# A GNN layer kernel: tail rows by SyncE, two tiles gathered raw, another order of scaling, and one loop for the last two batches

## Chip, cores and metric

One core of one Trainium2 chip. The metric is the device time of one execution in microseconds (us); the kernel before was run three times beside its profile.

## What is computed

A graph layer on 6250 nodes of 96 features and 106,250 edges that are sorted by their destination node. E is 830 tiles of 128 edges and a tail of 10.

```python
h = relu(layernorm(x))                                  # 6250 x 96
ea = edge_attr @ W_edge.T + b_edge                      # 106250 x 96
msg = relu(h[src] + ea)
aggr = segment_sum(msg, dst, num_segments=6250)
z = relu(((1 + eps) * h + aggr) @ W1.T + b1)
out = x + z @ W2.T + b2
```

## The kernel before

**Tiles and batches.** The 830 tiles are handled in 43 batches: 40 batches of 20 tiles (two sides of 10), then END with 16, LATE with 10 and LAST with 4. A side is a run of consecutive tiles; since edges are sorted, the nodes of one side fit into a window of 128 nodes or a few of them. For every tile three things come together: edge features (TensorE, in `edge_features_by_feature`, L505, for most batches, and in `edge_features`, L526, for the first and the last two), rows of the source nodes (a gather by GpSimd, L375), and a 0/1 matrix that says which edge goes to which node of the window (`make_select`, L771, on VectorE). For most batches the edge features come out transposed. ScalarE moves 32-wide blocks of them (`move_blocks`, L451), VectorE transposes within the blocks (`turn_blocks`, L926), adds the gathered rows (`add_rows`, L941), and takes the message apart into three bf16 parts with ScalarE's help (L458, L920, L463, L955). TensorE sums the messages by node (`sum_parts`, L604), and VectorE reduces the three parts (L853) and adds the turned sums of the window before into `acc` (`add_sums`, L825).

**The gathers.** Each gather fetches 128 rows of 384 bytes by a column of `src_all`. For batch 0 they come from `x` itself (20 gathers, in a burst of 13 and one of 7, the second after `norm_ready`), and VectorE normalises the gathered rows ("raw" tiles: `raw_var`, `raw_normalise`, in two parts of 10 tiles, `RAW_PARTS`). All other gathers, 810 and one of 10 rows for the tail (L388), read `h_table`, the normalised rows, which SyncE and ScalarE store to DRAM first; GpSimd waits for all of that store (`table_stored`) before the tail's gather. Two buffers `gathered` take turns. The gathers of batch c wait for two semaphores: `edge_begun` (TensorE's first matmul of features(c-1), which is issued after batch c-2 is used up) and `added` (VectorE's additions of batch c-2, by pairs of groups).

**Orders written out by hand.** Every engine has a program of its own. TensorE does, for each c: `turn_base(c-2)` (L552, for c of 2 to 14 only, which waits for ScalarE's blocks), `sum_windows(c-1)`, features(c+1). VectorE does: additions and parts of batch c, `sum_windows(c-1)`, `turn_blocks(c+1)`. SyncE issues the loads in this order: first source indices, x, weights, edges of batch 0, the table's stores, `dst_by_row`, `dst_all`, the tail's edges, edges of batch 1, five late weights; then, for each c from 2, edges of batch c once features(c-2) are done.

**The start on VectorE.** After the table: `raw_var(0)`; a wait for `dst_by_row` and its minimum (L764); `raw_normalise(0)` (L698, L699, ten of L756, L760); `raw_var(1)`; the maximum (L767); `raw_normalise(1)`. Then batch 0 is added (L941).

**The end.** The matrices of LATE and LAST are made ahead of need (`make_late_select`, L872), and the bounds of END, LATE and LAST are read into registers (nine `value_load`, L834 and L836). VectorE then does `add_rows(LATE)`, `sum_windows(END)`, `add_rows(LAST)`, `add_turned`, and a loop of its own for each of LATE and LAST over their windows, `sum_late_windows`: add two sides (L825), lower the offsets (L840), make the matrix of the next window (L872). TensorE has the matching loops (L613, and L616 for the tail's rows), with a `value_load` ahead of each. Then the two layers of the MLP follow in ten blocks of 625 nodes: z (L650), ReLU on ScalarE (L482), the result (L667), x added on VectorE (L997), stores (L361). TensorE's L650 of block 1 stands behind waits for `select_made` and both `late_selected` semaphores, since it writes the bank (`const_ps`) from which these matrices are made.

The sides' windows in this data end after one pass of each of the late loops.

```python
            for c in range(1, BATCHES):
                if c >= SLOTS:
                    pool.wait_ge(edge_begun, c)
                for p, (k0, k1) in enumerate(pairs[c]):
                    last_use = used_by(c, p, SLOTS)
                    if last_use is not None:
                        pool.wait_ge(added, adds_to[last_use] + p + 1)
                    for k in range(k0, k1):
                        gather(h_table, c, k)
```

## Time and profile before

| | |
|---|---|
| median of 3 runs | 1225.51 us (1225.41 to 1225.88) |
| the profiled execution | 1224.89 us |
| its span in the trace | 1223.1 us |
| granted TensorE clock, mean of the span | 0.673 of 2.4 GHz |
| busy: PE, VectorE, ScalarE, GpSimd | 41%, 50%, 42%, 64% of the span |
| HBM read, written | 87.85 MB, 4.80 MB |

The profiled execution's own time stands 1.8 us above its span and 0.6 us below the median. In the rows of the trace a line reads: start, duration, engine, line of the kernel, operation, written tile <- read tiles, shapes, count, and in brackets the idle time of the engine ahead of it and who ended that. "issue" means that nothing in the profile ended the wait, "remote" that a semaphore moved which the trace ties to no instruction close by. Rows of the same line that follow each other are merged. The duration of a DMA_INDIRECT row on POOL is what GpSimd is recorded to spend on issuing it, not its transfer.

### The profile page before, as it was taken

The numbers are of one execution on the slowest core, as the hardware profiler recorded it, in microseconds if no ns is written. First come the engines' busy times: TensorE is split into PE (matmuls) and PEld (weight loads), VectorE is DVE, ScalarE is ACT, GpSimd is POOL, SyncE is SP. The second block draws the span as 40 slices with busy tenths as digits, with TensorE's granted clock in tenths as the row PEclk, the third lists the DMA queues.
The fourth block names the chain that finished last, engine by engine and source line by source line (L and its number), as shares of the span: only waits on it lengthen the run. The fifth ranks groups of instructions, "written<-read, shape, count | busy, mean of one in ns | idle before, by whom it ended". The sixth has DMA issues, their size and how long they took to land.

```text
span 1223.1 us, 7306 instructions
## 1 busy us (share of the span) xinstructions
PE 496.0 (41%) x1592; PEld 249.7 (20%) x1592; DVE 607.6 (50%) x739; ACT 518.7 (42%) x713; POOL 785.8 (64%) x838
## 2 busy tenths in 40 slices
PE   2143344344344334245343253442534334425358
PEld 2011111222121112012111121120211111112146
DVE  6665544555554445364536345352545363543563
ACT  5134444344433335353435333343535343433434
POOL 6766666666666666575757575766757575757530
PEclk9967766767767766566666665666656666666669
DMA  7523333222223223242323332322423232322212
GB/s 217 148 66 71 83 78 68 67 68 68 67 67 68 68 68 98 56 112 71 81 71 80 72 79 64 72 68 61 101 54 82 63 72 64 71 64 67 47 28 79
DMA packets 51178, 93.18 MB, mean 76 GB/s; under 512 B 17722, under 2 KB 20443, under 8 KB 51136
## 3 DMA queue, kind: packets, MB, share of 16 engines
q0 software_dynamic: 26592, 40.85, 16.1%
q1 hardware_dynamic: 24390, 51.63, 15.6%
q8 instruction: 14, 0.23, 0.1%
q10 hardware_dynamic: 154, 0.24, 0.1%
q14 instruction: 28, 0.23, 0.1%
HBM read 87.85 MB, written 4.80 MB: 76 GB/s over the span
## 4 chain that ended last, share of the span: by engine, by line
another core or an unknown queue 32%; ACT 23%; issue 21%; DVE 13%; PE 6%; DVEq 4%; DMA 1%; SPq 0%; ACTq 0%
ACT edge_blocks L451 17%; ACT msg_parts L458 3%; DVE turn_ps L941 3%; DVE turn_ps L920 3%; PE turn_ps L505 2%; DVEq L834 2%; DVE turn_ps L926 2%; ACT msg_parts L463 2%; DVE msg_parts L955 1%; PE agg_ps L604 1%; PE turn_ps L667 1%; DVEq L836 1%; DVE stats L705 1%; DVE acc L825 1%
## 5 line engine op out<-in xcount | busy, mean ns | idle before, releaser
L375 POOL DMA_INDIRECT gathered<-h_table,src_all x810 | 764.4, 944 | 382.0 <-issue 237.7
L451 ACT COPY edge_blocks<-turn_ps 32x640 f32<-32x640 f32 (+1 forms) x480 | 325.9, 679 | 475.9 <-remote 358.8
L505 PE MATMUL turn_ps<-edge_in,w_edge 97*96 97x512 f32 x398 | 268.2, 842 | 324.2 <-issue 258.8
L926 DVE STREAM_TRANSPOSE turn_ps<-edge_blocks 128x960 f32<-128x960 f32 (+1 forms) x81 | 89.7, 1153 | 216.4 <-ACT edge_blocks L451 115.8
L853 DVE TENSOR_REDUCE sums<-agg_ps 128x192 f32<-128x576 f32 x41 | 30.9, 753 | 319.8 <-remote 319.8
L505 PEld LDWEIGHTS turn_ps<-edge_in,w_edge 97*96 97x96 f32 x398 | 88.6, 234 | 482.9 <-issue 482.9
L604 PE MATMUL agg_ps<-msg_parts,select 128*128 128x288 bf16 x816 | 155.6, 367 | 0.0
L458 ACT ACTIVATE msg_parts<-turn_ps 128x960 bf16<-128x960 f32 (+1 forms) x83 | 79.2, 957 | 157.2 <-DVE turn_ps L941 110.3
L771 DVE TENSOR_TENSOR select<-const_ps,dst_rel 128x2560 bf16<-128x2560 f32 (+1 forms) x43 | 120.8, 2812 | 33.2 <-issue 28.5
L604 PEld LDWEIGHTS agg_ps<-msg_parts,select 128*128 128x128 bf16 x816 | 103.4, 127 | 46.1
L941 DVE TENSOR_TENSOR turn_ps<-turn_ps,gathered 128x960 f32<-128x960 f32 (+1 forms) x83 | 91.1, 1144 | 2.1 <-DVE gathered L760 0.5
L920 DVE SCALAR_TENSOR_TENSOR turn_ps<-turn_ps,msg_parts 128x960 f32<-128x960 f32 (+1 forms) x83 | 91.1, 1144 | 0.3 <-ACT msg_parts L458 0.3
L955 DVE TENSOR_TENSOR msg_parts<-turn_ps,msg_parts 128x960 bf16<-128x960 f32 (+1 forms) x83 | 90.8, 1136 | 0.3 <-ACT msg_parts L463 0.3
L552 PE MATMUL turn_ps<-ident,h_all 125*96 125x125 f32 x50 | 13.1, 415 | 188.4 <-ACT edge_blocks L451 179.9
L567 PE MATMUL agg_ps<-ident,sums 128*96 128x128 f32 x84 | 23.6, 378 | 150.5 <-DVE acc L825 133.9
L463 ACT CAST msg_parts<-turn_ps 128x960 bf16<-128x960 f32 (+1 forms) x83 | 78.2, 945 | 11.6 <-issue 6.6
L552 PEld LDWEIGHTS turn_ps<-ident,h_all 125*96 125x96 f32 x50 | 7.9, 187 | 199.3 <-issue 199.2
L567 PEld LDWEIGHTS agg_ps<-ident,sums 128*96 128x96 f32 x84 | 10.3, 162 | 174.4 <-issue 171.7
L375 POOL DMA_INDIRECT gathered<-x_dram,src_all x20 | 19.6, 981 | 10.9 <-issue 5.5
L526 PE MATMUL turn_ps<-w_edge,edge_in 97*128 97x96 f32 x68 | 14.4, 406 | 27.1 <-DMA edge_in<-edge_t_dram 14.9
L825 DVE TENSOR_TENSOR acc<-acc,agg_ps 96x128 f32 x84 | 23.4, 279 | 0.9
L526 PEld LDWEIGHTS turn_ps<-w_edge,edge_in 97*128 97x128 f32 x68 | 13.9, 315 | 27.3 <-issue 27.3
(77 smaller groups left out, 187.9 us busy)
## 6 DMA issues: line engine op xcount, KB each, us to landing
edge_in<-edge_t_dram SPq DMA_DIRECT2D x165, 240.0 KB
gathered<-h_table,src_all POOLq DMA_INDIRECT x810
x_all<-x_dram SPq DMA_DIRECT2D x5, 420.0 KB
h_all<-x_dram SPq DMA_DIRECT2D x10, 210.0 KB
out_dram<-h_all SPq DMA_DIRECT2D x10, 210.0 KB
h_table<-h_all SPq DMA_DIRECT2D x3, 420.0 KB
h_table<-h_all SPq DMA_DIRECT2D x1, 630.0 KB
dst_by_row<-dst_rows_dram SPq DMA_DIRECT2D x1, 480.0 KB, 4.1
```

Source lines behind the costliest of these rows:

```text
L375: nc.gpsimd.indirect_dma_start(out=gathered[c % SLOTS][:, at:at + D], out_offset=None, in_=table, in_offset=bass.IndirectOffsetOnAxis(ap=s ...
L451: last = nc.scalar.copy(blocks[e:e + TURN, :, f:f + TURN], edges[f:f + TURN, :, e:e + TURN])
L458: last = nc.scalar.activation(in_parts(msg_parts[c % 2], a, b, 0), in_banks(c, a, b), ACT.Relu)
L463: last = nc.scalar.copy(in_parts(msg_parts[c % 2], a, b, 1), in_banks(c, a, b))
L505: mm = pe.matmul(turn_ps[0:D, q * BANK:q * BANK + (k1 - k0) * EDGE_TILE], w_edge[:], edge_in[c % SLOTS][:, k0 * EDGE_TILE:k1 * EDGE_TILE], ...
L604: mm = pe.matmul(agg_ps[:, s * BANK:s * BANK + SPLIT * D], select[c % 2][:, tile, :], msg_parts[c % 2][:, tile, :, :], start=(t == 0), sto ...
L771: nc.vector.tensor_tensor(select[b][:, 0:tiles, :], iota_ps.unsqueeze(1).broadcast_to((128, tiles, WINDOW)), dst_rel[:, bass.ds(at, tiles) ...
L825: return nc.vector.tensor_tensor(acc[:, cols], acc[:, cols], turned, ALU.add)
L920: return nc.vector.scalar_tensor_tensor(message, message, 0.0, high, ALU.max, ALU.subtract)
L926: last = nc.vector.transpose(in_flat(c, a, b), flat_rows(edge_blocks, a, b))
L941: last = nc.vector.tensor_tensor(put, in_banks(c, a, b), in_rows(gathered[slot], a, b), ALU.add)
L955: last = nc.vector.tensor_tensor(in_parts(msg_parts[c % 2], a, b, 2), in_banks(c, a, b), in_parts(msg_parts[c % 2], a, b, 1), ALU.subtract)
```

## The change

- **Tail rows by SyncE.** The tail's ten source indices come in as an input of their own (`tail_src`), are loaded into SBUF and from there into ten registers of SyncE, and SyncE issues ten DMAs of one row each from `h_table`. They stand behind the late weights and ahead of the edges of batch 2. GpSimd's L388 goes.
- **Two more raw tiles.** The first two tiles of batch 1 are gathered from `x` right behind batch 0's twenty, ahead of the wait for the table's store, and VectorE normalises them (a third raw part of two tiles).
- **Raw scaling ahead of the destinations by row.** VectorE does `raw_normalise(0)` and `raw_var(1)` before it waits for `dst_by_row`.
- **One loop for the last two batches.** LATE and LAST share one loop whose length is the longer of their two spans (one more reduction while the bounds are made); in it TensorE sums LATE, then LAST, and VectorE does the additions and offsets of both and then both comparisons. VectorE reads the bounds of LATE and LAST after `sum_windows(END)`, five loads instead of six.

```diff
-RAW_PARTS = ((0, 10), (10, 20))
+RAW_PARTS = ((0, 10), (10, 20), (20, 22))
+EARLY_TILES = 2
...
-            sp.dma_start(src_all[:, 0:tiles_of[0]], src_tiles[:, 0:tiles_of[0]]).then_inc(src_first_in, 16)
+            sp.dma_start(src_all[:, 0:RAW_TILES], src_tiles[:, 0:RAW_TILES]).then_inc(src_first_in, 16)
...
             load_edges(1)
+            sp.dma_start(tail_index[:], tail_src).then_inc(tail_index_in, 16)
             sp.dma_start(scale_eps[:], eps.rearrange("(a b) -> a b", a=1).broadcast_to((D, 1))).then_inc(late_weights_in, 16)
...
+            tail_row = [sp.alloc_register(f"sp_tail_row{k}") for k in range(TAIL)]
+            sp.wait_ge(tail_index_in, 16)
+            sp.load(tail_row, tail_index[0:1, 0:TAIL])
+            for k in range(TAIL):
+                node = sp.snap(tail_row[k], min_val=0, max_val=N - 1)
+                sp.dma_start(tail_gathered[k:k + 1, :], h_table[bass.ds(node, 1), :]).then_inc(tail_gather_in, 16)
...
             for k in range(FIRST_BURST, tiles_of[0]):
                 gather(x, 0, k)
+            for k in range(EARLY_TILES):
+                gather_early(k)
             pool.wait_ge(src_rest_in, 16)
             pool.wait_ge(table_stored, 16 * len(spread) * len(TABLE_PARTS))
-            nc.gpsimd.indirect_dma_start(
-                out=tail_gathered[:], out_offset=None, in_=h_table,
-                in_offset=bass.IndirectOffsetOnAxis(ap=src_all[0:TAIL, TILES:TILES + 1], axis=0),
-            ).then_inc(tail_gather_in, 16)
...
-                        gather(h_table, c, k)
+                        if c > 1 or k >= EARLY_TILES:
+                            gather(h_table, c, k)
...
-            def sum_late_windows(c):
...
+            def sum_late_windows(span):
                 with pe.Fori(0, span + 1, WINDOW):
+                    this_select = pe.snap(late)
+                    for c in (LATE, LAST):
+                        pe.wait_ge(late_relu_done, c - LATE + 1)
+                        if c == LAST:
+                            pe.wait_ge(tail_relu_done, 1)
+                        pe.wait_ge(late_selected[c], this_select)
+                        sum_rows(c).then_inc(late_summed, 1)
+                    pe.reg_add(window, window, 2)
+                    pe.reg_add(late, late, 1)
...
             raw_var(0)
+            raw_normalise(0)
+            raw_var(1)
             dve.wait_ge(dst_rows_in, 16)
             nc.vector.tensor_reduce(first_last[:, 0:1], dst_by_row[:], AX.X, ALU.min).then_inc(bounds_min_max, 1)
-            raw_normalise(0)
-            raw_var(1)
+            raw_var(2)
             nc.vector.tensor_reduce(first_last[:, 1:2], dst_by_row[:], AX.X, ALU.max).then_inc(bounds_min_max, 1)
-            ordered(raw_normalise(1))
+            raw_normalise(1)
+            ordered(raw_normalise(2))
...
+            def sum_late_windows(firsts, span):
                 with dve.Fori(0, span + 1, WINDOW) as done:
+                    for c in (LATE, LAST):
...
+                        dve.wait_ge(late_summed, this_late)
+                        dve.wait_ge(acc_summed, this_window)
+                        add_sums(0, cols[0], late_sums(c, 0)).then_inc(side_summed, 1)
+                        lower_offsets(first_tile[c], tiles_of[c] + (c == LAST)).then_inc(offsets_made, 1)
+                        dve.wait_ge(side_summed, this_window)
+                        add_sums(1, cols[1], late_sums(c, 1)).then_inc(acc_summed, 1)
+                    lowered, next_window = dve.snap(offsets), dve.snap(window)
                     dve.wait_ge(offsets_made, lowered)
                     dve.wait_ge(acc_summed, next_window)
-                    make_late_select(c)
+                    for c in (LATE, LAST):
+                        make_late_select(c)
...
-            end_bounds, late_bounds, last_bounds = (load_bounds(c) for c in (END, LATE, LAST))
+            end_bounds = load_bounds(END)
             add_rows(LATE)
             sum_windows(END, *end_bounds)
+            late_firsts, joint_span = {c: load_firsts(c) for c in (LATE, LAST)}, load_span(JOINT)
             add_rows(LAST)
             add_turned()
-            sum_late_windows(LATE, *late_bounds)
-            sum_late_windows(LAST, *last_bounds)
+            sum_late_windows(late_firsts, joint_span)
```

**GpSimd's whole program behind its constants**, before (L375 is a gather, L388 the tail's):

```order
L368 AFFINE_SELECT ident<-ident 128x128
L370 IOTA iota_sb 128x128
L375 DMA gathered<-x_dram,src_all 128x96 x20
L388 DMA tail_gathered<-h_table,src_all 10x96
L375 DMA gathered<-h_table,src_all 128x96 x810
```

and in the changed kernel:

```order
L384 AFFINE_SELECT ident<-ident 128x128
L386 IOTA iota_sb 128x128
L391 DMA gathered<-x_dram,src_all 128x96 x20
L398 DMA gathered<-x_dram,src_all 128x96 x2
L391 DMA gathered<-h_table,src_all 128x96 x808
```

The gathers from `h_table` go from 811 to 808, and two stand ahead of them, on the near side of the wait for the table's store.

**VectorE at the start**, before, from the minimum of `dst_by_row` on (`first_last`):

```order
L764 TENSOR_REDUCE first_last<-dst_by_row 96x1
L698 RECIPROCAL rstd<-std 128x10
L699 SCALAR_TENSOR_TENSOR shift<-mean,rstd 128x10
L756 TENSOR_SCALAR gathered<-gathered,rstd,shift 128x96 x10
L760 TENSOR_SCALAR gathered<-gathered 128x960
L745 BN_STATS raw_stats<-gathered 128x6 x10
```

and in the changed kernel, up to the same minimum (its L796) and the new tiles' statistics:

```order
L720 RECIPROCAL rstd<-std 128x10
L721 SCALAR_TENSOR_TENSOR shift<-mean,rstd 128x10
L786 TENSOR_SCALAR gathered<-gathered,rstd,shift 128x96 x10
L790 TENSOR_SCALAR gathered<-gathered 128x960
L771 BN_STATS raw_stats<-gathered 128x6 x10
L711 TENSOR_TENSOR gap<-raw_stats 128x10
L712 TENSOR_TENSOR spread<-raw_stats 128x10
L713 TENSOR_TENSOR mean<-raw_stats 128x10
L714 TENSOR_TENSOR gap<-gap 128x10
L715 SCALAR_TENSOR_TENSOR spread<-gap,spread 128x10
L796 TENSOR_REDUCE first_last<-dst_by_row 96x1
L775 BN_STATS raw_stats<-gathered 128x6 x2
```

The scaling of the first ten tiles and the statistics of the second ten moved ahead of the reduction that waits for `dst_by_row`.

**VectorE in the late loops**, before, from LATE's first addition to LAST's (ISA and REGISTER rows work on registers):

```order
L825 TENSOR_TENSOR acc<-acc,turn_ps 96x128
L840 TENSOR_SCALAR dst_rel<-dst_rel 128x10
L825 ISA
L825 TENSOR_TENSOR acc<-acc,turn_ps 96x128
L872 TENSOR_TENSOR late_select<-const_ps,dst_rel 128x1280
L879 ISA
L879 COMPARE_AND_BRANCH
L879 UNCONDITIONAL_BRANCH
L879 ISA
L828 ISA x2
L825 ISA
L825 TENSOR_TENSOR acc<-acc,turn_ps 96x128
```

and in the changed kernel, from LATE's second addition to the end of the loop's body:

```order
L859 TENSOR_TENSOR acc<-acc,turn_ps 96x128
L918 ISA
L862 ISA
L863 ISA
L859 ISA
L859 TENSOR_TENSOR acc<-acc,turn_ps 96x128
L878 TENSOR_SCALAR dst_rel<-dst_rel 128x5
L859 ISA
L859 TENSOR_TENSOR acc<-acc,turn_ps 96x128
L931 ISA
L910 TENSOR_TENSOR late_select<-const_ps,dst_rel 128x1280
L910 TENSOR_TENSOR late_select<-const_ps,dst_rel 128x640
```

LATE's comparison no longer stands between the additions of LATE and those of LAST; both comparisons stand behind them. On TensorE the second `value_load` and the loop's branch between LATE's matmuls and LAST's go.

## Rows read from the trace of the kernel before

**Rows 1.** The page: the group of the gathers (count; busy, mean ns; idle before)

```profile
L375 POOL DMA_INDIRECT gathered<-h_table,src_all x810 | 764.4, 944 | 382.0 <-issue 237.7
```

**Rows 2.** Timeline of POOL: its waits, with 20 and 40 gathers between them

```profile
120.62 0.94 POOL L375 DMA_INDIRECT gathered<-h_table,src_all  x1 [3.72 <-remote]
...
149.03 0.94 POOL L375 DMA_INDIRECT gathered<-h_table,src_all  x1 [3.75 <-remote]
...
574.47 0.94 POOL L375 DMA_INDIRECT gathered<-h_table,src_all  x1 [6.94 <-remote]
...
630.96 0.94 POOL L375 DMA_INDIRECT gathered<-h_table,src_all  x1 [6.86 <-remote]
```

**Rows 3.** Timeline, 130 to 149 us: TensorE's work and who starts after it

```profile
130.56 3.41 PE L604 MATMUL agg_ps<-msg_parts,select 128*128 128x288 bf16 x20
136.80 4.50 PE L505 MATMUL turn_ps<-edge_in,w_edge 97*96 97x512 f32 x10 [2.82 <-issue]
148.75 0.76 DVE L853 TENSOR_REDUCE sums<-agg_ps 128x192 f32<-128x576 f32 x1 [9.98 <-remote]
```

**Rows 4.** Timeline of POOL, the start and the first two runs of gathers

```profile
23.20 0.94 POOL L375 DMA_INDIRECT gathered<-x_dram,src_all  x1 [4.29 <-DVE shift L699]
26.94 1.54 POOL L375 DMA_INDIRECT gathered<-x_dram,src_all  x1 [0.30 <-issue]
31.28 0.94 POOL L375 DMA_INDIRECT gathered<-x_dram,src_all  x1 [0.30 <-issue]
34.43 0.88 POOL L388 DMA_INDIRECT tail_gathered<-h_table,src_all  x1 [2.21 <-DMA h_table<-h_all]
41.89 1.06 POOL L375 DMA_INDIRECT gathered<-h_table,src_all  x1 [0.30 <-issue]
60.77 0.94 POOL L375 DMA_INDIRECT gathered<-h_table,src_all  x1 [0.30 <-issue]
92.24 0.94 POOL L375 DMA_INDIRECT gathered<-h_table,src_all  x1 [6.81 <-remote]
```

**Rows 5.** Timeline of VectorE and SyncE, 26 to 51 us

```profile
26.75 0.91 DVE L736 TENSOR_SCALAR h_all<-h_all 125x1440 f32<-125x1440 f32 x1
37.67 1.48 DVE L764 TENSOR_REDUCE first_last<-dst_by_row 96x1 f32<-96x1280 int32 x1 [7.62 <-DMA dst_by_row<-dst_rows_dram]
39.30 1.72 SPq L320 DMA_DIRECT2D edge_in<-edge_t_dram  x4
39.52 2.62 DVE L756 TENSOR_SCALAR gathered<-gathered,rstd,shift 128x96 f32<-128x96 f32 x10
42.17 0.66 DVE L760 TENSOR_SCALAR gathered<-gathered 128x960 f32<-128x960 f32 x1
50.73 2.23 DVE L941 TENSOR_TENSOR turn_ps<-turn_ps,gathered 128x960 f32<-128x960 f32 x2 [0.51 <-DVE gathered L760]
```

**Rows 6.** Timeline of TensorE, features of batches 1 and 2

```profile
56.43 4.38 PE L505 MATMUL turn_ps<-edge_in,w_edge 97*96 97x512 f32 x5 [8.46 <-issue]
84.89 7.64 PE L505 MATMUL turn_ps<-edge_in,w_edge 97*96 97x512 f32 x10 [3.04 <-issue]
```

**Rows 7.** Line L834, VectorE's register loads: ns min/median/max, first and last start

```profile
L834 DVEq TENSOR_LOAD <-bounds_i x86: 298/303/547, 71.3 to 1183.5; - x86
```

**Rows 8.** Timeline, the end

```profile
1188.39 5.88 PE L613 MATMUL turn_ps<-late_select,gathered 128*96 128x128 f32 x28 [0.32 <-issue]
1193.92 1.49 DVE L872 TENSOR_TENSOR late_select<-const_ps,dst_rel 128x1280 f32<-128x1280 f32 x1
1195.74 0.28 DVE L825 TENSOR_TENSOR acc<-acc,turn_ps 96x128 f32 x1
1196.13 0.82 DVE L872 TENSOR_TENSOR late_select<-const_ps,dst_rel 128x640 f32<-128x640 f32 x1
1197.39 1.27 PE L650 MATMUL turn_ps<-acc,w 96*96 96x320 f32 x2
```

**Rows 9.** Busy time by stretch: us, PE busy, PEld, DVE, ACT, POOL, PEclk, DMA share, GB/s

```profile
1201.00:1217.00 16.00, 16.00 (x105) 13.03 (x104) 5.23 (x8) 9.94 (x15) 0.00 (x0) 1.00 0.34 106
```

More of the change, by code:

```diff
@@ L560, in _ @@
             selects = pe.alloc_register("pe_selects")
-            late = {c: pe.alloc_register(f"pe_late{c}") for c in (LATE, LAST)}
-            for c in (LATE, LAST):
-                pe.reg_mov(late[c], 1)
+            late = pe.alloc_register("pe_late")
+            pe.reg_mov(late, 1)
             def turn_sums():
@@ L640, in _ @@
                         edge_features(c + 1)
-            sum_late_windows(LAST)
             all_summed = pe.snap(window)
             all_selects = pe.snap(selects)
-            all_late = {c: pe.snap(late[c]) for c in (LATE, LAST)}
+            all_late = pe.snap(late)
             def hidden_sums(c):
```

95 lines of the change are left out of this document (52 added, 43 removed).

## The prediction

> **What bounds the kernel now.** I read the page first, then the timeline of GpSimd (POOL), then that of the other engines over one batch. No engine is busy for two thirds of the span on the page, and the chain of waits gives a third of it to an unknown releaser, so shares don't name the bound; the rhythm does. GpSimd's 810 gathers are 0.944 us each with 0.30 us between them [rows 1], 1.25 us from start to start, without a break over a batch; then it stops for 3.7 us once in 20 gathers, or for 6.9 us once in 40 [rows 2]. The period is 149.03 - 120.62 = 28.41 us for 20 gathers and 630.96 - 574.47 = 56.49 us for 40. Their difference gives 28.08 / 20 = **1.404 us for a gather**, and 28.41 - 28.08 leaves **0.33 us** for a stop. The stops are no slack, then: they are as long as the gathers ahead of them are many, and TensorE's clock and the other engines' work, which differ between the two patterns, do not show in the period.
>
> What ends a stop is odd. VectorE and GpSimd start within 0.3 us, at 148.75 and 149.03 [rows 2, 3], and both wait for TensorE, whose matmuls for them are modelled to have ended by 134.0 and 141.3 [rows 3]. TensorE's signals come when GpSimd's work would be done at 1.404 us a gather. I can't name the mechanism from this trace; I use the rule as measured. It holds at the start too: the first run of gathers begins with the tail's at 34.43 and has 1 + 40; 34.43 + 41 x 1.404 + 0.33 = 92.32, and the row says 92.24 [rows 4]. The Trainium skill (Perfetto Trace Analysis, DMA Instruction, SWDGE) says that the recorded end of such an instruction is when the last DSP has written its descriptors, and that the DSP finishes later. That would allow a true cost above 1.25 us, and the sum by 1.25 would be a gain of 3 x 1.25 instead of 3 x 1.40.
>
> So the forecast is about the number of gathers behind the table's store, and about what happens after the last stop.
>
> **Part 1: gathers.** 811 gathers stand behind the store; 808 will. At 1.404 us that is 4.2 us, if the first run began where it does now. It won't quite: two gathers more stand ahead of it. The burst now ends with the one issued at 31.28, and GpSimd then waits until 34.43 for the store [rows 4]. Two more steps of 1.25 us: the last early gather is issued at 33.78, the run of 38 begins at 35.03. Its stop ends at 35.03 + 38 x 1.404 + 0.33 = 88.7, 3.5 us earlier than 92.24. But if a gather really takes 1.404 us, the seven from 23.20 on and the two new ones carry their arrears into the run: 23.20 + 47 x 1.404 + 0.33 = 89.5, a gain of 2.7 us; and if the 0.6 us by which the gather at 26.94 was held up (1.54 for 0.94) comes on top, 90.1, a gain of 2.1 us. I take **2.7 us**, since the rule fitted every other run with arrears counted, and keep 2.1 and 3.5 as ends.
>
> Every later stop is set by the gathers alone, so this gain travels unchanged to the last one. What could eat it on the way:
>
> - Batch 2's gathers must not find `edge_begun` missing. They follow at 60.77 now and would at about 58. Features(1) begin at 56.43 [rows 6], right behind batch 0's messages. Those come earlier: L756 and L760 of the first ten tiles (39.52 to 42.83) and the statistics behind them move into the 7.62 us in which VectorE waits for `dst_by_row` [rows 5]. Against 3.3 us for the scaling alone stands the new pair of tiles, two tenths of it and some small operations; I take 2.5 us net, by which batch 0 starts before 50.73. Features(1) then begin near 54, and the cover is 4 us. Were it gone, each us missing would stop GpSimd for one. This part of the change is worth nothing by itself; it pays for part 1.
> - Features(2) end at 84.89 + 7.64 = 92.5 now, with the first stop [rows 6]; 2.5 us earlier is 90.0, beside 89.5. ScalarE's next copies could start 0.5 us late, but between the end of features at 141.3 and the release at 148.75 lie 7.4 us that would take it in [rows 3]; so nothing.
> - SyncE's ten rows. A DMA takes it 0.43 us to issue (four in 1.72) [rows 5]. Ten of them are 4.3 us; the ten registers are loaded, at 0.30 us each by VectorE's loads [rows 7], 3 us; 2 us stand for the wait for `tail_index`. The edges of batch 2 are then issued at about 49 for 39.30. TensorE wants them at 82, and the cover is over 30 us. The tail's rows themselves are wanted in batch 18. Nothing.
> - One more reduction of one row among the bounds on VectorE: under 0.3 us, ahead of matrices that wait less than the gathers do. Nothing.
>
> **Part 2: the end.** Behind the last long stop everything is a chain of the other engines. Now the last sum goes into `acc` at 1195.74 + 0.28 = 1196.0, and the second block of the MLP begins at 1197.39 [rows 8]. Six register loads fewer stand ahead of `add_rows(LATE)`, at 0.30 us or more each, 1.8 us at least, of which VectorE's comparisons cover some: L613 starts earlier by 0 to 1.8, I take 1.3, near the upper end. LAST's matmuls then follow LATE's as they do now (28 in one row), and no comparison of 1.49 us stands between the additions. The last sum is in at about 1194.7. But now both comparisons stand behind it, 1.49 + 0.82 = 2.3 us, and TensorE may not begin the second block before they are done: 1194.7 + 2.3 = 1197.0 to 1197.2, for 1197.39. **0.2 us** of 1.3 are left. Ends: a gain of 1.3 if the second block is not what matters, and a loss of 1.0 if the first ones fall into another stretch of TensorE's half clock.
>
> **Sum.** 2.7 + 0.2 = 2.9 us off the profiled execution's 1224.89 is 1222.0; the median of the runs is 0.6 above that execution, so **1222.6 us**. Own range of this case: 2.1 - 1.0 to 3.5 + 1.3, or 1220.7 to 1224.4.
>
> **A rule against the change.** The gather at 26.94 took 0.60 us more than the others while VectorE ran L736, a scaling of 0.91 us from SBUF to SBUF; L760 ran at 42.17 beside a gather of 1.06 us that began at 41.89, 0.12 us over the mean, and the mean over all 810 is the 944 ns of an undisturbed one [rows 1, 4, 5]. So one held GpSimd up and another hardly did, and the trace gives 0 to 0.6 us. Now the same L756 and L760 move under the early gathers, between 31 and 35 us, where GpSimd has no wait left to hide them.
> The Trainium skill (SBUF — State Buffer, Who interferes with whom) says that VectorE in a two-port mode, which `tensor_scalar` can take, locks GpSimd out wholly while it runs, so that descriptors aren't written. By that rule the move costs GpSimd all of 3.3 us.
>
> **Rivals.**
> 1. *Full price* (chance 0.15). The run starts at 35.03 with no arrears and the end gives its 1.3: 3.5 + 1.3 = 4.8, 1220.7 us. For it: GpSimd's recorded starts. Against: arrears fit the stops.
> 2. *Scaling locks GpSimd out* (0.10). L756 and L760 hold the early gathers for 2.62 + 0.66 = 3.3 us, the run starts at 38.3, the gain is 3.5 - 3.3 + 0.2 = 0.4: 1225.1 us. For it: the one row at 26.94. Against: the gather at 41.89.
> 3. *Gathers are not the bound* (0.13). The releases come from TensorE or from a process that has its own period, so three gathers fewer only lengthen a stop; the end's 0.2 is left: 1225.3 us. For it: "remote", and 3.7 us idle in 28.4. Against: the idle time doubles when the gathers do.
> 4. *The end loses* (0.07), slower. TensorE stands idle for a us ahead of the second block, and the MLP runs on at 1.2 GHz. At full clock it is TensorE's: 16.00 us busy in 16 us, 105 records, 14 to a block, 2.13 us a block [rows 9]. At half clock a block costs 2.13 more. Three blocks: 6.4 - 2.9 = 3.5 slower, 1229.0. It decides from 2.5 blocks on. Against: TensorE's load before and after is the same as now.
>
> That the change doesn't do what it says is not likely: the orders show the gathers moved.
>
> **How the numbers follow.** My case has 0.55. A measurement tells 0.2%, 2.45 us, from nothing, so the line lies at 1223.06, close to the forecast: within my case I give 0.70 to a gain above 2.45. Faster: 0.55 x 0.70 + 0.15 = 0.54. Same: 0.165 + 0.10 + 0.13 = 0.39. Slower: 0.07. The range reaches from rival 1 to rivals 2 and 3: 1220.5 to 1225.4, leaving out rival 4 and what lies beyond the ends.
>
> **What would show it.** Two early gathers at about 32.5 and 33.8, the first from `h_table` at 35.0, the first stop's end at 89.5 (88.7 by rival 1, 92 by rivals 2 and 3, where in 2 the early gathers are longer and in 3 the stop is). Periods of 28.4 and 56.5 as before. Batch 0 added near 48. All later ends of stops 2.7 us earlier, as 628.3 for 630.96. The last sum at 1192.0 and the second block of the MLP at 1194.5 (now 1196.0 and 1197.4). I am wrong if the stops' ends don't move with the gathers, if a stop appears before batch 2, or if the end moves by more than 1.3 us against the last stop.

## The result and the profile after the change

The changed kernel takes 1227.32 us (median of 22 runs, 1223.94 to 1230.45) against 1225.21 us for the kernel before in the same comparison (22 runs, 1223.77 to 1226.01): a ratio of **1.0022, 95% interval 1.0016 to 1.0028**. It is 2 us slower, by just about the 0.2% that a measurement can tell, and 4.7 us above the forecast. The execution that was profiled is the quickest of its 22: 1223.94 us, span 1222.1, for 1224.89 and 1223.1 before. So the two profiles alone would say "1 us faster"; what the median shows had to be looked for in more executions.

GpSimd's timeline of the changed kernel, the early gathers, the first from the table and the first two stops, which answer to [rows 2, 4]:

```profile
32.55 0.94 POOL L398 DMA_INDIRECT gathered<-x_dram,src_all  x1 [0.30 <-issue]
33.80 0.94 POOL L398 DMA_INDIRECT gathered<-x_dram,src_all  x1 [0.30 <-issue]
35.04 1.24 POOL L391 DMA_INDIRECT gathered<-h_table,src_all  x1 [0.30 <-issue]
...
90.77 0.95 POOL L391 DMA_INDIRECT gathered<-h_table,src_all  x1 [7.29 <-PE turn_ps L527]
...
119.23 0.95 POOL L391 DMA_INDIRECT gathered<-h_table,src_all  x1 [3.76 <-remote]
```

The early gathers and the run's start are where they were forecast (32.5, 33.8, 35.0). The early two take 0.94 us while VectorE scales raw tiles beside them (ten of L786, 32.07 to 34.77); only the gather at 35.04 is 0.30 us longer, beside L790 (34.81 to 35.47). The period is 119.23 - 90.77 = 28.46 us, as before. But the first stop ends at 90.77, not 89.5, and its releaser is no longer "remote" [rows 4] but TensorE's features. Its timeline has their start, which answers to [rows 6]:

```profile
88.50 7.42 PE L527 MATMUL turn_ps<-edge_in,w_edge 97*96 97x512 f32 x10 [3.27 <-issue]
```

They begin 3.6 us later than before, not 2.5 earlier. VectorE's timeline between batch 0's messages and the matrices shows where the chain loses its lead (batch 0 was added at 47.22, 3.5 us earlier than before):

```profile
54.44 0.23 DVE L813 TENSOR_TENSOR span_f<-bounds_f 1x96 f32<-1x96 f32 x1
56.97 0.24 DVE L816 TENSOR_REDUCE span_f<-span_f 1x48 f32<-1x96 f32 x1 [2.29 <-remote]
58.35 0.14 DVE L817 TENSOR_REDUCE span_f<-span_f 1x1 f32<-1x2 f32 x1 [1.15 <-DVE span_f L816]
59.06 0.18 DVE L819 CAST bounds_i<-span_f 1x48 int32<-1x48 f32 x1 [0.56 <-issue]
...
68.23 5.55 DVE L803 TENSOR_TENSOR select<-const_ps,dst_rel 128x2560 bf16<-128x2560 f32 x2 [7.73 <-remote]
```

VectorE's timeline of the kernel before has the same steps:

```profile
57.92 0.23 DVE L781 TENSOR_TENSOR span_f<-bounds_f 1x96 f32<-1x96 f32 x1
58.19 0.24 DVE L784 TENSOR_REDUCE span_f<-span_f 1x48 f32<-1x96 f32 x1
58.47 0.17 DVE L785 CAST bounds_i<-span_f 1x48 int32<-1x48 f32 x1
...
64.63 5.56 DVE L771 TENSOR_TENSOR select<-const_ps,dst_rel 128x2560 bf16<-128x2560 f32 x2 [4.72 <-remote]
```

Operations of 0.2 us, each waiting for the one before it on the same engine, start 2.5, 1.4 and 0.7 us apart, where they were 0.3 us apart before. From the first of them to the offsets that follow (57.92 to 58.56 before, 54.44 to 59.16 now) that makes 4.1 us more, of which only 1.4 lie between the added reduction (L817) and the step ahead of it. The matrices wait 7.73 us for 4.72, another 3.0.

The end, TensorE's and VectorE's timeline, which answers to [rows 8]:

```profile
1185.76 2.40 PE L634 MATMUL turn_ps<-late_select,gathered 128*96 128x128 f32 x20
1190.38 1.11 PE L634 MATMUL turn_ps<-late_select,gathered 128*96 128x128 f32 x8 [2.22 <-ACT gathered L495]
...
1193.44 2.35 PE L672 MATMUL agg_ps<-acc,w 96*96 96x320 f32 x4 [1.56 <-DVE acc L859]
1195.76 1.35 PE L672 MATMUL turn_ps<-acc,w 96*96 96x320 f32 x2
...
1197.93 2.34 PE L689 MATMUL turn_ps<-w,x_all 97*125 97x128 f32 x10
1200.06 1.33 PE L672 MATMUL agg_ps<-acc,w 96*96 96x320 f32 x4
...
1189.21 0.56 DVE L980 TENSOR_TENSOR gathered<-turn_ps,gathered 128x384 f32<-128x384 f32 x1 [1.11 <-issue]
...
1193.01 0.28 DVE L859 TENSOR_TENSOR acc<-acc,turn_ps 96x128 f32 x1
1193.40 2.22 DVE L910 TENSOR_TENSOR late_select<-const_ps,dst_rel 128x1280 f32<-128x1280 f32 x2
```

The last sum is in at 1193.3, 2.7 us earlier than the 1196.0 before. But the MLP's third block starts at 1200.06, only 1.0 us earlier than before (1201.10): the first blocks are slow. The stretches with TensorE's clock (us, PE busy, PEld, DVE, ACT, POOL, PEclk, DMA share, GB/s) say why:

```profile
1190.00:1193.00 3.00, 1.50 (x10) 1.14 (x10) 1.30 (x6) 0.33 (x1) 0.00 (x0) 1.00 0.00 0
1193.00:1200.00 7.00, 6.56 (x18) 4.30 (x19) 2.50 (x3) 3.29 (x4) 0.00 (x0) 0.53 0.00 0
1200.00:1205.00 5.00, 5.00 (x32) 4.04 (x31) 1.63 (x3) 2.80 (x4) 0.00 (x0) 0.97 0.32 98
```

The granted clock is 0.53 while the MLP starts, the lower of its two levels (1.2 GHz), behind a stretch with two waits (2.22 and 1.56 us) in which TensorE was half idle.

### The profile page after: what moved, and what is told of

The parts are those of the page before. It is cut to its first block, busy times and chain, and to the rows that moved or that the text cites. A ratio compares the mean times of both kernels' runs of the same rounds, so it can differ in the third digit from the quotient of the medians.

```text
span 1222.1 us, 7340 instructions
## 1 busy us (share of the span) xinstructions
PE 495.8 (41%) x1592; PEld 248.0 (20%) x1592; DVE 610.0 (50%) x752; ACT 519.2 (42%) x714; POOL 787.7 (64%) x837
## 4 chain that ended last, share of the span: by engine, by line
another core or an unknown queue 31%; issue 25%; ACT 24%; DVE 11%; PE 4%; DVEq 4%; DMA 0%; ACTq 0%; SPq 0%
ACT edge_blocks L473 19%; ACT msg_parts L480 3%; DVE turn_ps L959 3%; DVE turn_ps L980 3%; ACT msg_parts L485 2%; DVEq L868 2%; DVE turn_ps L965 2%; PE turn_ps L527 1%; DVE msg_parts L994 1%; PE turn_ps L689 1%; DVEq L872 1%; DVE stats L727 1%; DVE acc L859 1%; PE agg_ps L625 1%
## 5 line engine op out<-in xcount | busy, mean ns | idle before, releaser
L803 DVE TENSOR_TENSOR select<-const_ps,dst_rel 128x2560 bf16<-128x2560 f32 (+1 forms) x43 | 120.8, 2812 | 36.6 <-issue 28.9
```

What stands on the lines that cost most here:

```text
L803: nc.vector.tensor_tensor(select[b][:, 0:tiles, :], iota_ps.unsqueeze(1).broadcast_to((128, tiles, WINDOW)), dst_rel[:, bass.ds(at, tiles) ...
```

## The experiments

Three places could hold the loss, and the expectations call them by letters where they need one: R, SyncE's ten rows; S, the start up to the first stop (from e5_only_joint on also F, the features of batch 2 in it, with a rival O, the order of scaling); E, the end. Every kernel was timed beside the kernel before on the same chip. The chips differed: on three of them (here A, B, C) the kernel before takes 1224.9, 1224.9 and 1232.8 us and GpSimd stops in every period; on the fourth, D, used twice, it takes 1082.1 and 1080.8 us, and it doesn't. So each time is compared with the kernel before on its own chip, by the ratio. The changed kernel itself did not run on D.

| label | chip | median us | ratio, 95% interval |
|---|---|---|---|
| e1_again | A | 1226.85 | 1.0020, 1.0011 to 1.0028 |
| e2_tail_pool | A | 1227.47 | 1.0020, 1.0011 to 1.0029 |
| e3_rows_later | A | 1228.29 | 1.0029, 1.0019 to 1.0039 |
| e4_only_rows | A | 1224.01 | 0.9993, 0.9984 to 1.0002 |
| e5_only_joint | D | 1084.42 | 1.0018, 1.0009 to 1.0028 |
| f2_only_order | D | 1083.01 | 1.0008, 0.9999 to 1.0017 |
| f3_only_early | D | 1083.90 | 1.0015, 1.0006 to 1.0024 |
| e9_acc_by_act | D | 1083.30 | 1.0017, 1.0008 to 1.0026 |
| k1_again | B | 1227.53 | 1.0018, 1.0008 to 1.0029 |
| h1_old_end | B | 1223.78 | 0.9995, 0.9984 to 1.0005 |
| h2_kept_busy | B | 1225.67 | 1.0008, 0.9998 to 1.0017 |
| j1_rows_busy | B | 1222.63 | 0.9986, 0.9977 to 0.9995 |
| j2_again | D | 1078.68 | 0.9981, 0.9972 to 0.9990 |
| m2_all_but_joint | D | 1077.03 | 0.9970, 0.9958 to 0.9982 |
| n1_ten_fewer | D | 1076.95 | one execution; before 1080.78 |
| e8_nineteen | D | 1036.19 | one execution; before 1080.78 |
| o1_all_but_joint | C | 1232.64 | 0.9995, 0.9983 to 1.0007 |
| o2_ten_fewer | C | 1231.52 | 0.9994, 0.9978 to 1.0010 |

**e1_again**: the changed kernel as it is.

> The changed kernel once more, unchanged, for a profile of a typical execution. Theory R (rows): SyncE takes some 3.7 us for each of the ten rows while gathers run (36.6 us in the profile of the change), so the edges of batch 2 are issued at 81.4 us or later instead of 39.3, and features(2) and GpSimd's first stop wait for them in most executions. Expected: about 1227 us, and in the profile edges of batch 2 issued at 81 to 88 us, first stop of GpSimd ended at 91 to 96 us, each later one later by the same. Theory E (end): the joint loop or the clock behind it loses time; the first stop then ends at 90.8 as in the first profile of the change, and the stretch from the last stop to the end is 3 us longer than 84. Theory S (scaling): raw scaling under the early gathers delays the first gather from the table; it then starts at 37 to 39 instead of 35.0.

It repeats, 1.0020. Its profiled execution, 1223.44 us, is again its quickest. It shows another course of the start: batch 0 is added at 51.42 and features(1) begin at 58.76, not near 54, and GpSimd's timeline has a stop ahead of batch 2, one of the prediction's own signs of being wrong:

```profile
61.02 0.95 POOL L391 DMA_INDIRECT gathered<-h_table,src_all  x1 [3.33 <-PE turn_ps L527]
```

**e2_tail_pool**, the changed kernel with the tail gathered by GpSimd:

```
-            for k in range(TAIL):
-                sp.dma_start(tail_gathered[k:k + 1, :], h_table[bass.ds(node, 1), :])...
+            nc.gpsimd.indirect_dma_start(out=tail_gathered[:], in_=h_table, ...)
```

> The change without the rows by SyncE: GpSimd gathers the tail again, first behind the table's store; the rest of the change stays. Theory R: edges of batch 2 issued at 39 us again, all excess gone; two gathers fewer behind the store than before against 1.6 us of later start, so 1223.5 to 1225.0, 0.2 to 1.5 us under before. Theories E and S: 1227 as the change.

**e3_rows_later**, the rows behind the loads of the edges of batches 4 to 13, one each:

```
             load_edges(c)
+            if 4 <= c < 4 + TAIL:
+                sp.dma_start(tail_gathered[c - 4:c - 3, :], h_table[bass.ds(node, 1), :])...
```

> The change with the ten rows issued one a batch, behind the edges' loads of batches 4 to 13, and the registers loaded behind those of batch 3. Theory R: nothing waits for a row any more, so faster than before and than the change: 1222 to 1224. If a row by SyncE costs by its mere traffic or by its number, 1227 stays. Theories E and S: 1227.

**e4_only_rows**, the kernel before with SyncE's rows alone, the tail's gather out.

> The kernel before with the rows by SyncE alone (no early tiles, old order at the start, two late loops). Theory R: edges of batch 2 issued at 80 us or later, batch 0 3.5 us later than in the change, one gather less: 1226 to 1229 and a spread of some us between executions. Theories E and S: 1224, one gather less than before and nothing else.

R falls: without the rows, or with them elsewhere, the loss stays at 0.2 to 0.3%, and alone they are the one part whose ratio is under 1 (0.9993, less than a gather's worth, and not clear of 1). They do cost SyncE far more than forecast. Its timeline in the changed kernel:

```profile
44.17 36.55 SPq L363 DMA_DIRECT2D tail_gathered<-h_table  x10
81.41 16.27 SPq L328 DMA_DIRECT2D edge_in<-edge_t_dram  x12
```

The ten take 36.55 us and not 4.3, and the next edges are issued at 81.4, not at 49. That eats the whole cover of 30 us and shows nowhere in the time. On chip D, where GpSimd doesn't stop, the ten take 4.06 us (j2_again, m2_all_but_joint).

**e5_only_joint**, **f2_only_order**, **f3_only_early**: the kernel before with one part each (the joint loop and its bounds; scaling ahead of the destinations by row; the two early tiles in the old order).

> The kernel before with the joint late loop alone (and its one reduction more among the bounds). Theory F (features of batch 2): SyncE's rows are cleared by the runs so far; in three profiles of slow executions GpSimd's first stop ends 1.3 to 2.3 us behind the start of features(2), which come at 88.5 to 91.5 instead of 84.9, because VectorE's small instructions inside the first run of gathers are held up (steps of 1.4 us, and 7.7 us in one piece ahead of the first select matrix). What adds small instructions there costs; the joint loop adds one: 1225 to 1226, first stop's end within 1 us of 92.2. Theory E (end): the joint loop is the loss: 1227.5, with 84.9 us or more from the last long stop to the end instead of 83.6.

> The kernel before with the raw scaling of the first ten tiles and the statistics of the next ten ahead of the wait for the destinations by row, and nothing else. Theory F: no instruction is added, batch 0 is added 5 us earlier; features(2) follow only in part, and the first stop is set by the gathers: 1224.5 to 1225.5. Rival O: the order itself moves VectorE's small steps into a stretch in which they are held up (7.7 us ahead of the select matrix instead of 4.7) and the gain is eaten: select matrix at 68 to 71 us, 1226 to 1228.

> The kernel before with the two early raw tiles alone, in the old order of scaling, tail by GpSimd, two late loops. Theory F: some fifteen small VectorE instructions more in the first run; batch 0 added 2 us later, features(2) 2 to 6 us later: 1226 to 1228. Rival O (the order): 1224 to 1225, two gathers fewer behind the store.

On chip D the gathers come 1.25 us apart all the way. The page's group of e5_only_joint has 246.9 us of idle time for the 382.0 of [rows 1]:

```profile
L384 POOL DMA_INDIRECT gathered<-h_table,src_all x810 | 764.6, 944 | 246.9 <-issue 245.6
```

The joint loop alone costs 2.3 us there, so it is at fault even where no stop is. The order alone (f2) is at 1.0008, not clear of 1; its profiled execution, 1078.54 us, is its quickest, 4.5 us under its median. TensorE's timeline has the first and the third block of the MLP in e5_only_joint:

```profile
1052.56 2.37 PE L669 MATMUL agg_ps<-acc,w 96*96 96x320 f32 x4 [0.99 <-DVE acc L854]
...
1058.89 1.22 PE L669 MATMUL agg_ps<-acc,w 96*96 96x320 f32 x4
```

and in f2_only_order, which keeps the old end:

```profile
1051.24 1.26 PE L650 MATMUL agg_ps<-acc,w 96*96 96x320 f32 x4 [2.01 <-DVE acc L825]
...
1054.76 1.22 PE L650 MATMUL agg_ps<-acc,w 96*96 96x320 f32 x4
```

6.33 us apart against 3.52. The early tiles alone cost too, 1.8 us: in the old order their scaling and statistics stand ahead of batch 0, features(1) begin at 55.1, and GpSimd waits for them. Its timeline in f3_only_early:

```profile
57.38 1.69 POOL L380 DMA_INDIRECT gathered<-h_table,src_all  x1 [2.61 <-PE turn_ps L520]
```

**e9_acc_by_act**, the changed kernel with `acc` cleared by ScalarE, not by VectorE's operation of 5.37 us in the chain of the start:

```
-                nc.vector.memset(acc[:], 0.0).then_inc(acc_summed, 1)
+            nc.scalar.activation(acc[:, 0:3360], h_all[0:D, 0:3360], ACT.Relu, scale=0.0)
```

> The change, with acc cleared by ScalarE at 31 us (two activations with scale 0) instead of by VectorE's memset of 5.4 us ahead of batch 1. Theory F: the chain to features(2) is 5 to 6.5 us shorter, so features(2) start before 86 and the first stop is set by the gathers again, at 89.5 to 91: 1222.5 to 1224.5 and a narrow spread. Theory E, or any cause that does not run through VectorE's chain to features(2): 1227 as the change.

A miss. The clearing went ahead of ScalarE's `std` for the raw tiles, so VectorE's scaling waited 7.03 us for it, and GpSimd again waited 2.60 us for features(1). It says nothing about what clearing costs in the chain, nor can its 1.0017 be set beside the changed kernel, which has no time on D.

**k1_again, h1_old_end, h2_kept_busy, j1_rows_busy**, four on chip B. h1 is the changed kernel with the end of the kernel before. h2 is the changed kernel with products that nobody reads in TensorE's two waits; j1 is e4_only_rows with such products ahead of the turned sums and of the MLP:

```
+            def keep_busy(n):
+                for _ in range(n):
+                    pe.matmul(prep_ps[:, 0:128], ident[:], ident[:], start=True, stop=True)
...
+                            keep_busy(16)
                         pe.wait_ge(late_relu_done, c - LATE + 1)
...
+            keep_busy(10)
             pe.wait_ge(acc_summed, all_summed)
```

> The changed kernel unchanged, timed beside the next three on one chip, since it isn't given that the chip is the one of the earlier runs. All theories: 1.0015 to 1.003 times the kernel before. Theory E (the end): its MLP begins at TensorE's half clock, the granted clock between the last sum and the second block's start is 0.5 to 0.6, and from the first product with w1 to the next block's lie over 6 us. Theory S (the start): the MLP costs what it costs in the kernel before, and the loss is there by the end of the first run of gathers.

> The changed kernel with the end of the kernel before (a loop for each of the last two batches, comparisons between the additions); SyncE's rows, two early tiles and the new order stay. Theory E: the loss is the joint loop's, so this is 1.5 to 3 us faster than the changed kernel, 0.998 to 1.0005 of the kernel before. Theory S: it stays at 1.0015 to 1.003.

> The changed kernel with products that nobody reads (ident by ident, 128 columns, into a bank that is free) in TensorE's two waits of the end: 16 between the last two batches' sums and 10 ahead of the MLP. Theory E with the clock as its cause: the MLP begins at full clock, its first two blocks are about 3.5 us apart instead of over 6, and the time falls by 2 to 3 us against the changed kernel, to 0.9985 to 1.0005 of the kernel before. If the waits themselves and not the clock make the loss, nothing is won, or 0.5 us is lost. Theory S: the MLP's start gains, but the changed kernel's 1.002 falls by no more than it would in the kernel before, where some 1.4 us of the first block are at half clock too.

> The kernel before with SyncE's ten rows instead of the tail's gather (alone 0.9993 of the kernel before) and with such products in two waits of TensorE at the end: 10 ahead of the turned sums, 10 ahead of the MLP. Candidate to beat both kernels. Clock as the cause: the stretch of half clock at the end (L613's 28 products took 5.9 us, the first block 4.9 us to the second) shrinks, 1.5 to 3 us less than the rows alone, 0.997 to 0.998. If the products only delay the real ones: 0.9993 to 1.0005.

Without the joint loop the loss is gone: 1223.78 for 1227.53. The stretch from the last sum to the MLP's third block in k1_again, by its clock:

```profile
1197.00:1204.00 7.00, 6.76 (x19) 4.52 (x20) 2.32 (x3) 3.28 (x4) 0.00 (x0) 0.51 0.00 0
```

in h1_old_end:

```profile
1198.70:1202.40 3.70, 3.55 (x19) 2.46 (x20) 0.82 (x1) 2.56 (x4) 0.00 (x0) 1.00 0.00 0
```

and in h2_kept_busy:

```profile
1200.00:1204.20 4.20, 4.20 (x27) 2.99 (x26) 1.59 (x2) 2.56 (x4) 0.00 (x0) 1.00 0.00 0
```

19 products take 6.8 us at a clock of 0.51 and 3.55 us at 1.00. The products of h2 make the clock 1.00 without changing what the end computes, so the clock is the cause of the slow first blocks. TensorE's timeline in h2_kept_busy shows their price (each product of ident is two of the 32 and 20 records):

```profile
1193.42 3.74 PE L611 MATMUL turn_ps<-ident 128*128 128x128 f32 x32
1196.99 1.04 PE L640 MATMUL turn_ps<-late_select,gathered 128*96 128x128 f32 x8
...
1198.34 2.50 PE L611 MATMUL turn_ps<-ident 128*128 128x128 f32 x20
1200.67 1.22 PE L678 MATMUL agg_ps<-acc,w 96*96 96x320 f32 x4
...
1204.14 1.22 PE L678 MATMUL agg_ps<-acc,w 96*96 96x320 f32 x4
```

They hold up the last 8 products to 1196.99 and the MLP to 1200.67, 1.4 us behind the last sum at 1199.25. So 3.1 us of blocks are won and some 2 given back: 1.1 us are left by the traces' ends below, 1.9 us by the medians (1.0008 for 1.0018, not the 0.9985 to 1.0005 that was expected).

From the end of END's edge features to the end of the span, over all the executions profiled, the end has three prices (worked out as the span less the start of the last row `edge_blocks<-turn_ps` of ScalarE, which in every trace begins 0.03 to 0.05 us behind the last product `turn_ps<-edge_in,w_edge`):

| end | executions | us |
|---|---|---|
| joint loop | after, e1, e2, e3, k1, e5, e9 | 61.4, 61.8, 62.2, 61.5, 61.4, 62.3, 61.4 |
| joint loop, kept busy | h2 | 60.3 |
| old end | before, e4, o2 | 61.8, 61.8, 61.8 |
| old end | h1, f2, f3, n1, e8 | 59.8, 59.4, 59.8, 59.4, 59.7 |
| old end, kept busy | j1, j2, m2, o1 | 59.4, 59.3, 59.4, 59.4 |

The old end meets the half clock in the MLP in three of eight executions (before, [rows 8], was one: L613's 28 products in 5.88 us, and 4.93 us from the first block to the third) and misses it in the others; the joint one has met it in all seven. The three are all on chips with stops, where only h1 misses it; none is on D. So against the first kind the joint end is between 0.4 us better and 0.5 worse, against the second it loses 1.6 to 2.9, and the comparison of the two profiles showed the first.

h1_old_end also bears on what the joint row of bounds costs at the start. VectorE's timeline there:

```profile
61.41 0.24 DVE L815 TENSOR_REDUCE span_f<-span_f 1x48 f32<-1x96 f32 x1 [1.58 <-remote]
62.81 0.17 DVE L816 CAST bounds_i<-span_f 1x48 int32<-1x48 f32 x1 [1.16 <-DVE span_f L815]
...
71.98 5.56 DVE L802 TENSOR_TENSOR select<-const_ps,dst_rel 128x2560 bf16<-128x2560 f32 x2 [7.71 <-remote]
```

and in k1_again:

```profile
60.45 0.24 DVE L816 TENSOR_REDUCE span_f<-span_f 1x48 f32<-1x96 f32 x1 [1.60 <-remote]
61.85 0.14 DVE L817 TENSOR_REDUCE span_f<-span_f 1x1 f32<-1x2 f32 x1 [1.16 <-DVE span_f L816]
63.25 0.18 DVE L819 CAST bounds_i<-span_f 1x48 int32<-1x48 f32 x1 [1.26 <-DVE span_f L817]
...
72.41 5.55 DVE L803 TENSOR_TENSOR select<-const_ps,dst_rel 128x2560 bf16<-128x2560 f32 x2 [7.72 <-remote]
```

One more step is 1.40 us here, and it stands in the chain that ends the first run of gathers in both. The ends of the stops are only 0.7 us apart (94.28 and 94.95, behind features(2) at 92.25 and 92.68), since batch 0 was added 0.9 us later in h1 (49.96 and 49.02). No kernel has the added reduction alone, so its price is read from the steps and not tested.

**j2_again** (j1 once more) and **m2_all_but_joint** (h1_old_end with j1's products: all of the change but the joint loop), both on chip D, and **o1_all_but_joint** (m2 once more), on chip C.

> The kernel before with SyncE's ten rows and the products that keep TensorE busy at the end, once more, as the base of the next one. 0.998 to 0.9995 of the kernel before, as measured before it: 0.9986.

> j2_again with the two early tiles and the new order in it, so all of the change but its joint loop, and the products. If a gather taken out of the first run is worth 1.40 us (the step of the prediction that gave 2.7 us for three, of which two are in question here): 2 us faster than j2_again, 0.997 of the kernel before. If the first run's end is set by the chain of batch 0, the matrices and features(2), which got two tiles' work longer and lost the wait for dst_by_row: within 1 us of j2_again, 0.998 to 0.9995.

> m2_all_but_joint once more, for a chip on which the gathers' stops are there; on the one without them it was 0.997 of the kernel before and 1.65 us faster than j2_again. If two gathers fewer behind the store count everywhere: 2 us under j1_rows_busy (0.9986), 0.997. If on a chip with the stops the chain of the other engines ends the first run, as the traces of the changed kernel there say (features(2) begin at 88 to 93, the stop ends 1.3 to 2.3 us behind): 0.998 to 0.9995, no better than j1_rows_busy.

The early tiles in the new order give 1.65 us where GpSimd doesn't stop (1078.68 to 1077.03), and with the other parts 0.3% under the kernel before. On a chip with stops the same kernel is 0.9995, for j1's 0.9986 on another: no gain from them that can be seen. j1 itself fell short of its 0.997 to 0.998, and since e4's 0.9993 is from another chip, what the products alone are worth there isn't shown.

**n1_ten_fewer** and **o2_ten_fewer**: the kernel before without ten gathers of batch 2 (older rows stand in for them).

```
-                        gather(h_table, c, k)
+                        if c != 2 or k < 10:
+                            gather(h_table, c, k)
```

> The kernel before without ten of batch 2's twenty gathers (its sums are those of older rows), so the first run has 31 for 41. By the rule of 1.404 us a gather its stop would end at 34.4 + 31 x 1.404 + 0.3 = 78.3 instead of 92.2. By the chain: features(2) can't begin before about 80 (batch 0 added at 50.7 and 29.6 us of other work behind it, as on the chip without stops), so the stop ends at 82 to 86, and the time falls by 6 to 10 us. If the waits that VectorE's small operations show in this run come from the gathers queued behind GpSimd, those behind 73 us vanish. If neither gathers nor chain set it, it stays at 92.

> n1_ten_fewer once more, for a chip with the stops. On the one without them it took 3.8 us off, features(2) began at 76.8 and the stop ended 3.1 us behind. With the stops: if VectorE's and TensorE's signals are held up by the gathers queued behind GpSimd's issue (1.25 us to issue, 1.40 a gather), the chain is held up less with ten gathers fewer, features(2) begin at 78 to 84 instead of 85 to 93, and 6 to 12 us go. If the chain has other reasons to be late there, features(2) begin where they do with all gathers and 0 to 4 us go.

GpSimd's timeline in o2_ten_fewer, and then TensorE's:

```profile
85.50 0.94 POOL L375 DMA_INDIRECT gathered<-h_table,src_all  x1 [12.16 <-issue]
```

```profile
83.30 6.20 PE L506 MATMUL turn_ps<-edge_in,w_edge 97*96 97x512 f32 x10 [2.32 <-DVE msg_parts L956]
```

The rule of 1.404 us says 78.6, the row says 85.5: 2.2 us behind the start of features(2), with GpSimd idle for 12.16 us ahead of it. Ten gathers are worth 3.8 us on D (one execution) and, by the ratio, 0.7 us on C, between 2.7 won and 1.2 lost. With ten gathers fewer it is the chain that ends the first run. With the changed kernel's three fewer it is so in most of the executions profiled, not in all.

**e8_nineteen**: the kernel before without the twentieth gather of batches 2 to 39.

> The kernel before without 38 gathers, the twentieth of batches 2 to 39 (older rows stand in for them). Rule of 1.404 us a gather: 19 of them to a period of 28.4 - 1.4 = 27.0 us, 53.4 us off the whole. By the recorded 1.25 us: 47.5. If the other engines' chain of a batch is the bound, or a period of its own, much less. On a chip that has no stops at 1.25 us a gather: 47.5, and periods of 23.7.

1036.19 for 1080.78: 44.6 us for 38 gathers, 1.17 each, so on chip D they are the bound at nearly their recorded 1.25 us. The rule of 1.404 us for the later runs was not tried on a chip with stops.

## Why the prediction was wrong

By its own steps:

- **Gathers and where they stand**: right. 808 behind the store, the early ones at 32.55 and 33.80, the run from 35.04. Periods as before. The scaling doesn't lock GpSimd out for 3.3 us (0.94 us beside L786, 0.30 more beside L790): rival 2 falls.
- **"Its stop ends at 89.5, a gain of 2.7 us"**: the failed step. A law fitted to runs in which the gathers end last was used one step past the point where they still do. The forecast had features(2) end 0.5 us behind the stop and called that nothing; but a stop ends 1.3 to 3.1 us behind the *start* of features(2) wherever these are late (after 90.77 - 88.50 = 2.3, n1 79.92 - 76.81 = 3.1, o2 85.50 - 83.30 = 2.2), and they were late in six of the eight executions of the changed kernel and its variants on chips with stops: they began at 88.5 to 93.4, and only in e1_again and o1 at 86.1 and 87.8. In these two features(1) were late instead (58.76 and 63.90), and GpSimd stopped for 3.33 and 6.39 us ahead of batch 2. The gain (against the one profile of the kernel before) was 1.5 us in the profiled execution, 2.2 in e1_again, -1.4 in e2_tail_pool and -2.7 in k1_again; the last two are the executions nearest to the changed kernel's median (1227.51 and 1227.74 us). The prediction's 2.7 us is in none.
- **"Features(1) near 54, batch 0 2.5 us earlier"**: right in the profiled execution (52.9, 3.5 us), not in e1_again (58.8), and worth nothing, since the steps behind it were held up. Unhindered, batch 0 to features(2) takes 29.6 us (f2, 40.28 to 69.83); before took 34.2, the changed kernel 41.3, k1_again 43.7.
- **"One more reduction: under 0.3 us, nothing"**: mis-sized. Its step takes 1.40 us in k1_again and 1.38 in the profiled execution, on the chain (0.28 in e1_again). It was priced by its length; the engine also waits for its own last result.
- **SyncE's ten rows**: costed at 9 us in all, 4.3 of them for the rows, measured 42 and 36.6 (batch 2's edges at 81.4 for 39.3); "nothing" was right all the same (e2, e3, e4).
- **"The last sum 1.3 us earlier"**: against the last features it is 2.1 us earlier (33.3 us behind their last product's start, 35.4 before). Better than forecast. But that the MLP's start would keep its pace was wrong: **"0.2 us are left"** is, against h1 on the same chip, a loss of 1.6 us by the traces' ends (61.4 and 59.8), and 2.9 on chip D (e5 62.3, f2 59.4), where the joint loop alone measured 2.3. Against the profile of the kernel before it is a gain of 0.4 (61.8): that execution had a half clock of its own.
- **Rival 4** (0.07), the half clock at the end, is what happened, in a smaller size: 3.1 us for the first two blocks against a full clock, not three blocks more on top, with 2.1 us of earlier sums against it. I held against it that TensorE's load was the same; what counted was its idle time. By the order of the code it is the register loads, moved ahead of `add_rows(LAST)`, that open a wait of 2.22 us in the middle of TensorE's 28 products, where the old order has none (before, h1) or 0.62 (j1); no run moved them alone.

- **Rivals 1 and 3**: 1 falls with the stops' ends. 3 holds for the first run, and by another mechanism than it named: the idle time is there (12.16 us in o2), but a chain sets it. For the later runs it falls on chip D (e8) and is untested on a chip with stops.

The sum by what was measured: without the joint loop and its reduction the change is at 0.9995 (h1), some 0.6 us of gain for the 2.7 forecast, and not clear of none. With them it is at 1.0018 (k1), 3.75 us more by the medians (2.8 by the ratios, with some 1.8 either way), for the 0.2 of gain forecast. So the joint loop and its reduction turn the change into a loss; how much of that lies at the start and how much at the end is less sure. The two profiled executions are only 1.6 us apart (spans of 1225.9 and 1224.3), 0.7 of it by the first stop's end. From the first stop's end to the end of the span the changed kernel took 1131.3, 1131.6 and 1131.0 us in its three profiled executions (1222.1 - 90.77, 1221.6 - 90.03, 1225.9 - 94.95), h1 1130.0 and the kernel before 1130.9. So what differs between these three was made by the first stop's end; that the whole spread of the changed kernel's times (1223.4 to 1230.5 us) has this source is an inference. An estimate from these figures, for the medians less 1.8 us to get spans: the first stop ends at 1225.7 - 1131.0 = 94.7 in k1 and at 1222.0 - 1130.0 = 92.0 in h1, so 2.7 of the 3.75 would be lost at the start and 1 us behind it. The added reduction's step would explain 1.4 of the 2.7. On chip D, without stops and without such spacing of VectorE's steps, the joint loop's 2.3 us go with an end that is 2.9 us longer (e5 against f2).

What stays open: whether the 1.4 us are paid in most executions on chips with stops, and what else the start loses; why the old end meets the half clock in three of four executions there and in none on D; why VectorE's steps are spaced by 1.4 us in some executions and not in others (in before, o2, e1_again, e4_only_rows and o1 they are mostly 0.3 apart).

A version beats both kernels, by just about what can be told: j1_rows_busy, 0.9986 and 0.9981 on two chips. With the early tiles it is 0.9970 on D, 0.9995 on C.

## What to carry to other kernels

When a law says which of two processes ends a stretch, work out by how much the other one is behind; a gain is worth no more than that distance, and any operation added to the second counts in full from there. Moving work out from between two waits of TensorE can cost more than it frees, if the waits then come close together ahead of a stretch in which it is the bound: look at the granted clock of that stretch first, and at whether a few products nobody reads bring it back. And one profile of each kernel is two executions: if the range of a kernel's times is wider than the effect, take several.

## What the runs showed of the hardware

- The same kernel takes 1081 us on one chip and 1225 to 1233 us on the others. Most of the difference is GpSimd's stops: 246.9 us idle (e5_only_joint) for 382.0, that is 135 of 144 us; the gathers' 0.944 us are the same.
- On the chips with stops, SyncE's three instructions for a row start 1.4 us apart each during a run of gathers (in the changed kernel from 49 us on; its ten rows take 18.9 to 37.6 us on these chips, 4.06 on D), and VectorE's dependent small steps 1.40 us apart in many executions. That is close to the 1.404 us that the prediction read as the cost of a gather; that it is the same thing is not shown. The matrices' wait, up to 7.76 us there, is nought on chip D:

```profile
51.97 0.24 DVE L821 TENSOR_REDUCE span_f<-span_f 1x48 f32<-1x96 f32 x1
52.25 0.17 DVE L822 CAST bounds_i<-span_f 1x48 int32<-1x48 f32 x1
...
53.79 5.56 DVE L808 TENSOR_TENSOR select<-const_ps,dst_rel 128x2560 bf16<-128x2560 f32 x2
```

  (VectorE's timeline in m2_all_but_joint; no wait is named in it.) On the chips with stops it is 1.50 us, none and none in the three executions in which GpSimd stopped for over 3 us ahead of batch 2 (e1_again 3.33, e4_only_rows 5.07, o1 6.39), and these have the shortest times for the ten rows too (23.0, 19.6, 18.9 us). So signals of several engines are late together while gathers are under way. That they share one path is a guess.
- 26 small products (16 and 10, h2_kept_busy) keep TensorE's clock at 1.00 through two waits of 2.2 and 1.6 us, behind which it otherwise is 0.51 for 7 us (k1_again).
